# Second layer of a four-part block on one core: background pauses and rates, the ranks' third product, and a counter kept by GpSimd

## What is computed

```python
# selective scan, 512 inner channels, 16 states
x_ssm, res = split(x @ W_in.T); x_ssm = silu(causal_conv(x_ssm, taps of 4) + b_conv)
dt = softplus(x_ssm @ W_dt.T + b_dt);  B = second half of x_ssm @ W_x.T
h = exp(dt * A) * h + dt * B * x       # for each token, channel and state
y = (h.sum(states) + D * x) * silu(res);  out = y @ W_out.T
# router of the expert groups
scores = softmax(x2 @ router_w); weights, experts = top_k(scores, 2)
xs = x2[tokens sorted by expert]
```

## Time and profile before

| | |
|---|---|
| time, median of 3 runs | 5053.47 us (5053.16 to 5054.25) |
| time of the profiled execution | 5061.28 us |
| its span, first to last instruction | 5059.5 us |
| instructions | 58338 |
| busy share of the span: PE, DVE, ACT, POOL | 87%, 76%, 50%, 60% |
| second layer's scans | about 2596 to 4361 us |
| one chunk of it | 97 us (the first), then 109 to 116 us, the last 100 |

### The profile page before, as it was taken

One profiled execution on the slowest core, in us unless ns is written; L12 is line 12 of the kernel. 1 busy time (PEld: TensorE's weight loads), 2 busy tenths in 40 slices (PEclk: granted clock), 3 DMA queues, 4 the chain that ended last, 5 costly groups with the idle time before them and its releaser, 6 DMA issues.

```text
span 5059.5 us, 58338 instructions
## 1 busy us (share of the span) xinstructions
PE 4382.1 (87%) x18832; PEld 2875.0 (57%) x18832; DVE 3830.7 (76%) x6231; ACT 2543.8 (50%) x4769; POOL 3022.2 (60%) x1972
## 2 busy tenths in 40 slices
PE   4789999899899899899988888989888888489994
PEld 1355555555555555555655555555555555378883
DVE  6898767788767788766148888888888888645677
ACT  1334333334333334333557777777777766245552
POOL 4455444555444455444156888888788888745552
PEclk7899999999999999999989999999999998699997
DMA  4233332333322333322111221111122111496787
GB/s 142 84 101 110 99 96 84 100 98 109 98 90 90 98 100 107 98 89 89 57 70 55 83 74 69 71 65 64 64 82 84 64 65 65 151 237 206 252 272 279
DMA packets 302509, 545.46 MB, mean 108 GB/s; under 512 B 30592, under 2 KB 146560, under 8 KB 293248
## 3 DMA queue, kind: packets, MB, share of 16 engines
q1 hardware_dynamic: 274560, 466.08, 28.5%
q0 software_dynamic: 27648, 75.67, 4.1%
HBM read 422.71 MB, written 118.92 MB: 107 GB/s over the span
## 4 chain that ended last, share of the span: by engine, by line
PE 52%; DVE 23%; ACT 10%; POOL 7%; issue 5%; DMA 2%; SPq 0%; DVEq 0%; POOLq 0%; another core or an unknown queue 0%; ACTq 0%
PE psum L207 20%; PE psum L794 6%; DVE a_S L896 5%; PE psum L1902 5%; POOL c_dbx L1419 4%; PE psum L669 4%; DVE c_hs L1437 4%; PE psum L1161 4%; DVE a_prod L902 3%; PE psum L1453 3%; PE psum L1925 3%; PE psum L1209 2%; PE psum L918 2%; ACT psum L1426 2%; POOL sorted_rows L1376 1%
## 5 line engine op out<-in xcount | busy, mean ns | idle before, releaser
L1419 POOL TENSOR_TENSOR c_dbx<-c_dtx,c_Brep 128x1024 f32<-128x1024 f32 x512 | 1202.3, 2363 | 265.6 <-DVE c_hs L1437 210.2
L1437 DVE TENSOR_TENSOR_SCAN c_hs<-psum,c_carry,c_dbx 128x512 f32<-128x512 f32 x768 | 934.8, 1264 | 149.6 <-ACT psum L1426 117.6
L887 POOL TENSOR_TENSOR a_kv<-a_rk,a_kv 128x512 f32<-128x512 f32 x512 | 790.4, 1557 | 398.3 <-DMA a_kv<-v_rows 397.8
L813 POOL TENSOR_TENSOR a_hid_e<-a_hid_e,a_g_rep 128x512 f32<-128x512 f32 x256 | 376.8, 1475 | 868.7 <-ACT a_hid_e L802 624.4
L896 DVE TENSOR_TENSOR_SCAN a_S<-a_decay,a_carry,a_kv 128x513 f32<-128x513 f32 x512 | 813.9, 1590 | 62.6 <-POOL a_kv L887 56.6
L1426 ACT ACTIVATE psum<-c_dt,c_cols 128x512 f32<-128x512 f32 x1024 | 694.1, 687 | 297.0 <-DVE c_hs L1437 289.6
L1453 PE MATMUL psum<-ident,c_hs 128*128 128x128 f32 x4096 | 649.5, 296 | 156.7 <-DVE c_hs L1437 152.1
L1453 PEld LDWEIGHTS psum<-ident,c_hs 128*128 128x128 f32 x4096 | 515.4, 152 | 412.7 <-DVE c_hs L1437 242.1
L902 DVE TENSOR_TENSOR a_prod<-a_rk,a_S 128x512 f32<-128x512 f32 x512 | 515.0, 1006 | 186.0 <-PE psum L918 185.8
L794 PE MATMUL psum<-a_W_down,a_hid_e 128*128 128x256 f32 x2304 | 561.8, 390 | 51.0 <-DVE a_xb L826 24.2
L207 PE MATMUL psum<-a_xT,a_W_up 128*128 128x512 f32 x1152 | 557.8, 614 | 47.2 <-ACT a_hid_e L802 47.1
(11 more groups left out here) (267 smaller groups left out, 6999.5 us busy)
## 6 DMA issues: line engine op xcount, KB each, us to landing
a_kv<-v_rows SPq DMA_DIRECT2D x512, 256.0 KB
a_g_rep<-g_rows SPq DMA_DIRECT2D x256, 256.0 KB, 3.8
c_Brep<-b_rows SPq DMA_DIRECT2D x64, 1024.0 KB
d_xs<-sorted_rows SPq DMA_DIRECT2D x320, 128.5 KB
d_w<-results SPq DMA_DIRECT2D x64, 512.0 KB, 11.4
d_w<-in_d_experts SPq DMA_DIRECT2D x32, 768.0 KB
sorted_rows<-d_zeros SPq DMA_DIRECT2D x66, 128.5 KB, 11.0
a_xa<-in_L_attn_x SPq DMA_DIRECT2D x16, 512.0 KB, 4.5
```

What stands on the lines that cost most here:

```text
L887: m_kv[g] = pool.mark(nc.gpsimd.tensor_tensor(kv[:, g % NV, 1:C + 1], rk[slot][:, 1, hb, :], kv[:, g % NV, 1:C + 1], ALU.mult))
L1419: m_dbx[g] = m_dbx[g + 1] = pool.mark(nc.gpsimd.tensor_tensor(dbx[:, r:r + 2, :], dtx[slot][:, e, :].unsqueeze(1).broadcast_to([P, 2, C]), ...
L1437: m_scan[q] = dve.mark(nc.vector.tensor_tensor_scan(hs[:, q % NR, :], psum[:, DA + q % ND, :], dbx[:, q % NX, :], first, ALU.mult, ALU.add))
```

## The change

In `before`, ACT's Silu of the convolution comes `LAG + 1` = 3 background steps after PE's last product where it came 1 after, and ACT's reading of a step size 3 where it was 2. The ranks' product comes 2 steps after DVE's additions where it was 1. The rates of `after_scan` and `before` go from 1.15 and 1.15 to 1.2 and 1.3.

The expert's beginning is now added by PE: a third pair of one row of ones and `route.room`, in the bank of the ranks, except in the last chunk, where DVE adds it. With that L1355 goes, and the cast L1549 that fed it.

The number of the result row is written by DVE in the first two chunks alone. From the third on `sort_rows` waits for the transfers of two chunks before, and POOL adds a constant (`two_chunks`, set once by DVE) to what is there.

```diff
@@ before
-                yield
+                yield from pause(LAG + 1)
                 for e, i, bank, m in held:
                     act.after(m, *scanned)
                     m_xs[e] = G.freed[i] = act.mark(nc.scalar.activation(xs_[:, e, :], bank, ACT.Silu, bias=b_conv[:, e, :]))
@@ step_size
                 m = pe.mark(m)
-                yield from pause(LAG)
+                yield from pause(LAG + 1)
@@ after_scan
-            dve.mark(nc.vector.tensor_scalar(xn_[:, :, D], token_row[:, :], float(c * C * TOP), None, ALU.add))
+            if c < 2:
+                dve.mark(nc.vector.tensor_scalar(xn_[:, :, D], token_row[:, :], float(c * C * TOP), None, ALU.add))
...
-            yield
+            yield from pause(LAG)
             i, bank = yield from G.claim(pe)
...
-            m_rank = m_done["yT free", c] = pe.mark(matmuls(nc, ranks, [(tri[:, :], R["chosen"][:, :, :].rearrange("p r e -> p (r e)")),
-                                                                       (ones[:, :], ahead[:, 0:TL, :].rearrange("p t e -> p (t e)"))]))
+            pairs = [(tri[:, :], R["chosen"][:, :, :].rearrange("p r e -> p (r e)")), (ones[:, :], ahead[:, 0:TL, :].rearrange("p t e -> p (t e)"))]
+            if c < NCH - 1:
+
+                pairs.append((ones[0:1, :], route.room[0:1, :].unsqueeze(1).broadcast_to([1, TL, NE])))
+            m_rank = m_done["yT free", c] = pe.mark(matmuls(nc, ranks, pairs))
...
+                m = dve.mark(nc.vector.tensor_tensor(moved, moved, route.room[:, :].unsqueeze(1).broadcast_to([P, TL, NE]), ALU.add))
+                dve.after(m)
...
-            dve.after(m)
-            m = dve.mark(nc.vector.scalar_tensor_tensor(out=place[:, :, :, :].rearrange("p t g k -> p (t g) k"), in0=R["index_f"][:, :, :], scalar=float(Z.pitch),
-                                                        in1=place[:, :, :, :].rearrange("p t g k -> p (t g) k"), op0=ALU.mult, op1=ALU.add))
@@ sort_rows
-            pool.after_alone(*m_done["placed", c])
+            m_row = None
+            if c >= 2:
+
+                pool.engine.wait_ge(s_sorted[c % 2], c // 2 * per_chunk)
+                m_row = pool.mark(nc.gpsimd.tensor_tensor(route.xn[c % 2][:, :, D], route.xn[c % 2][:, :, D], two_chunks[:, :], ALU.add))
+            pool.after_alone(*m_done["placed", c], m_row)
@@ rates
-        AFTER_RATE, BEFORE_RATE, SORT_RATE, AHEAD = 1.15, 1.15, 0.4, 2
+        AFTER_RATE, BEFORE_RATE, SORT_RATE, AHEAD = 1.2, 1.3, 0.4, 2
@@ router
     m = dve.mark(nc.vector.tensor_copy(picks, R["index"][:, :, 0:top]))
-    dve.mark(nc.vector.tensor_copy(R["index_f"][:, :, :], R["index"][:, :, 0:top]))
```

## The result

The changed kernel takes 5024.35 us (median of 4 runs, 5021.03 to 5027.1), the kernel before 5053.86 beside it: 29.5 us less, a ratio of 0.9937 (95%: 0.9924 to 0.9951). Forecast were 5019.5 us and 34 less. The two profiled executions are 40.2 us apart (span 5059.5 and 5019.2), 32.6 of them between the first and the last scan of the second layer, where the change acts. The other 7.7 lie before and behind it, where the profiles of all these kernels differ by such amounts (the first scan starts between 2589.2 and 2601.4 us, though what stands ahead of it is the same in all), so 32.6 is what there is to explain.

What follows compares the result with a forecast made beforehand. The bound was taken to move inside a chunk: POOL nearly full first, PE from step 16 to 35, then DVE. Terms -20 - 4 - 11 - 3.5 + 5 = -33.5, say -34 us, from 5053.5 to 5019.5; range 4988 to 5048.

Steps and rivals of the forecast that it cites:

- Part 1, the reads: ScalarE's reads of PE's products sit 1 to 2 scan steps later: -20 us at the convolution, -4 at the step sizes.
- The terms of -20 and -4: Later reads: 1.3 us in 15 chunks at the convolution (bounds 0, -36), 0.3 a chunk at the step sizes (0, -15).
- rival A: ScalarE's wait for PE at the convolution only moves to the gate; DVE's edits leave -10, 5043 us; chance 0.20.
- Part 2, L1301 to L1303: DVE's L1301 removed, but L1303 behind it waits for the same end of POOL's multiplication: 0, bounds 0 and -23 us.
- Part 2, L1355 and L1549: DVE's removed instructions after step 43: L1355 -3.5 us (bounds -5, +5), cast L1549 -11 us (bounds -11, 0).
- The rates: Higher background rates hardly compress PE's work, since the second projection waits for a bank; PE's program stays as it is.
- Part 3: PE's third product for the ranks, at step 46: cost 0, hidden by DVE's work; +16 us if that cover is gone.
- Part 4: POOL's added instruction in sort_rows, 1.1 us with its wait, counting only in the first piece: +5 us, bounds 0 and +18.
- rival C: POOL becomes the bound, DVE waits for it over 25 us: slower, +18, 5071 us; chance 0.11.
- B: Cover is better: L1301's wait really vanishes, L1303 staying at 0.16, or two scans are won: about 5000 us; chance 0.17.
- D: Steps don't shift because banks run out, all parts lost in each other: within 5 us of 5053; chance 0.07.

Runs made afterwards that it cites:

- e1: Kernel before with the lengthened pauses and the rates 1.2 and 1.3, none of the edits on DVE, PE and POOL: 5063.57 us, ratio 1.0011.
- e6: Changed kernel with the result row's number written by DVE in every chunk and POOL's addition gone: 5032.04 us, ratio 0.9942 to the kernel before.
- e7: Changed kernel with the reciprocal of the total written to PSUM: 5030.73 us, ratio 0.9935 to the kernel before.
- e9: Changed kernel with reciprocal, chosen counts and places in PSUM, two small copies on ScalarE: 4997.23 us, ratio 0.9898 to the kernel before.
- e2: Changed kernel with the old pauses and rates put back, so the edits alone: 5059.28 us, ratio 1.0009 to the kernel before.
- e5: Changed kernel with the expert's beginning added by DVE again (L1355, L1549 back, PE's third product out): 5059.57 us, ratio 0.9999 to the kernel before.
- e3: Kernel before with the rates 1.2 and 1.3 alone: 5113.58 us, ratio 1.0114.
- e8: Changed kernel with the old rates, 1.15 and 1.15: 5032.37 us, ratio 0.9939 to the kernel before.
- e10: Same as e9 but with the old rates, 1.15 and 1.15: 4974.27 us, ratio 0.9856 to the kernel before.
- e4: Kernel before with the lengthened pauses alone, rates kept at 1.15: 5030.93 us, ratio 0.9948.

## Why the prediction was right, and where not

**Total and sign: right.** Forecast -34, measured -29.5 by the medians and -32.6 in the stretch. The terms stand less well.

**Part 1, the reads: size right, place partly wrong.** The exponentials sent before each read are now 27 and 37 at the convolutions, 40 and 44 at the gate, 47, 50, 54, 57 at the step sizes (before: 26 and 35, 39 and 43, and the same four). That is the count by hand, step for step. The terms of -20 and -4 stand against 240.2 - 215.2 = 25 us of idle time won, and e1 shows it without the edits (27). By place, DVE's idle time in all chunks fell from 82.8 to 28.7 us behind the scans 32 to 35, where the second convolution is read, and rose by 19 behind 36 to 39, by 6 behind 40 to 43 and by 10 behind 12 to 15. The convolution's wait fell to 14.5, as forecast under 35. But the gate's wait did not grow (11.0 to 7.0). I had overlooked the read between the two gates: the B projection's copy stays at 41 exponentials, while the first gate's read ahead of it comes one later. Its place in the changed kernel, in the timelines of ScalarE, PE and DVE:

```profile
3292.09 0.69 ACT L1434 ACTIVATE psum<-c_dt,c_cols 128x512 f32<-128x512 f32 x1
3294.51 0.57 ACT L1199 COPY c_tmp<-psum 16x512 f32<-16x512 f32 x1 [1.73 <-PE psum L207]
```

```profile
3290.86 3.61 PE L207 MATMUL psum<-c_xs,c_W_B 128*16 128x512 f32 x8
```

```profile
3295.70 1.28 DVE L1445 TENSOR_TENSOR_SCAN c_hs<-psum,c_carry,c_dbx 128x512 f32<-128x512 f32 x1 [0.97 <-ACT psum L1434]
```

ScalarE has sent one exponential since the gate and stands 1.73 us until PE's product is over at 3294.47; DVE then stands 0.97. DVE's wait for exponentials fell further than forecast (108 for 145), and the difference was given back: where ScalarE is no longer late PE is, and DVE waits for its transposes at step 36 (23.3 us) and for the output projection at step 16 (12.3 us). That is rival A's mechanism in small, at three places that I had not named.

**Part 2, L1301 to L1303: right.** The wait passed to the next instruction as forecast, 2.6 to 24.6 us, and e6 puts it, together with POOL's addition, at nothing (ratio 0.9942 for 0.9937). This is the rule of the Trainium skill that the prediction drew on ("SBUF — State Buffer", section "Who interferes with whom": an exclusive lock on the shared ports, taken by two SBUF inputs or by copy and cast in a two-port mode). e7 and e9 agree with it: the same operation took 0.17 us with one input in PSUM and, in most of its places, 1.85 with two in SBUF, both 0.53 to 0.55 us behind POOL's start.

**Part 2, L1355 and L1549: near as a difference of two kernels, mis-sized as parts.** Forecast -3.5 and -11. Between the two profiles the lines that the edits touch fell by about 18 us (L1301 -21.2, L1549 -12.7, L1355 -5.8, the weights +22.0, the cast to the row -1.0, the comparison behind L1549 +0.9), -14.5 being forecast, and DVE's busy time, in which neighbours that overlap count once, by 7.6. By themselves the edits are worth nothing with the old timing (e2), their 11 us coming back as idle time, while with the new timing (e5) L1355 and L1549 are worth all 30. The weak step is the costing of each part by the durations of the kernel before. I took L1355 at 5.8 us though one long case showed that its length is a matter of when it comes (there is a second, 1.32 us at 4353.24); the pauses, in the same change, moved it, and it would have taken 28.0 (e1). So the parts don't add up: pauses and rates alone 1.0011, edits alone 1.0009, both 0.9937. The total came out near because L1355 is gone in the changed kernel, and with it what the pauses do to it, and because the instructions behind it do not wait (e5). Of this the prediction weighed only the cast behind L1355, so that much is luck. The instructions' own work is only 7.7 us (14 and 16 of them at 0.16, 16 at 0.17).

**The rates.** I held them for neutral because the bank claims pin PE's program. e3 refutes that for ScalarE: the rates pull its reads forward, by up to four exponentials, at a cost of 55 us. PE's program is pinned up to the second convolution only (its last products come when 34 scans have begun, for 35 before); the step sizes' products begin at 40 for 43. In the changed kernel the rates make up for the longer pauses and are not needed (e8).

**Part 3: right.** The third product stands nowhere in the waits; DVE's wait for the places' bank is 4.0 us. PE's wait for the counts fell from 29.4 to 2.2 instead of staying; I take that to be without effect, as DVE is full there.

**Part 4: too high.** The addition is 0.21 us and its wait 9.9 us in 11 times, 0.9 each as forecast, but the 5 us of cost do not show: without it (e6) the idle time is 1.5 us less. DVE's waits for POOL went from 13.7 to 18.1, under the 25 of rival C.

**The rivals.** B's L1303 at 0.16 did not come, C did not decide, D fell. A holds in part, as said.

Open: how much of e10's further 23 us is the later reads, how much the other spread of PE's work that e4 showed, and how much TensorE's clock, below.

## What to carry to other kernels

A small DVE instruction that meets a long GpSimd one costs what its place and its operands make it, not what its size says; look for short forms with long durations, and for the next such form behind them, before a removal is costed. Removing such an instruction hands the wait on where the next one is of a waiting form (L1301 to L1303, L1304 to the copy), and ends it where the next ones have an operand in PSUM (L1355); giving every small form in reach such an operand ended it everywhere but in two instructions. Where an in-order engine reads another's results, try delaying the reads before raising the rate of the background, and time changes of order and edits together: here the pauses with their rates, and the edits, were each worth nothing alone.

## What the runs showed of the hardware

The size of a contending instruction hardly matters: 128x4, 128x16 and 128x64 forms all stood until POOL's end (1.96 us at 0.41 us behind its start, 1.86 at 0.53, 1.77 at 0.63). In 107 places, in ten profiles, a scalar_tensor_tensor of 128x16 with two inputs in SBUF began between 0.42 us ahead of POOL's multiplication and 1.42 behind its start; every one of them ended 2.37 to 2.42 us behind that start. A reciprocal of 128x8 within SBUF stayed at 0.19 us through POOL's multiplications: in the changed kernel the one at 3298.78 began 1.72 us behind POOL's start and 0.64 ahead of its end. POOL's indirect DMA instruction, 1.03 us long, did not hold DVE: in the changed kernel L1304 took 0.17 us at 4083.41, with that instruction running from 0.15 us before to 0.87 behind its start, and 33 such places in the profiles show 0.17 to 0.26 us.

TensorE's granted clock differs with how the background is spread: its mean over the execution is 0.930 before, 0.932 in the changed kernel and 0.943 in e10. Windows at the end of the same chunk, before (steps 56 to 59, 60 to 63, and 0 to 3 of the next) and then e10 (the same steps), columns as in the earlier trace rows:

```profile
3348.77:3354.67 5.90, 2.62 (x16) 1.68 (x16) 5.90 (x8) 4.71 (x10) 5.71 (x4) 1.00 0.58 200
3354.67:3361.18 6.51, 4.00 (x16) 2.56 (x16) 6.37 (x14) 3.38 (x8) 4.85 (x3) 0.57 0.80 261
3361.18:3366.46 5.28, 5.01 (x24) 4.78 (x24) 5.28 (x7) 3.35 (x6) 4.97 (x4) 0.56 0.00 0
```

```profile
3308.75:3314.63 5.88, 5.88 (x27) 3.46 (x26) 5.88 (x7) 5.85 (x11) 4.71 (x2) 1.00 0.07 26
3314.63:3320.77 6.14, 6.14 (x28) 3.53 (x27) 6.02 (x7) 6.11 (x13) 4.68 (x2) 1.00 0.66 252
3320.77:3327.25 6.48, 4.71 (x30) 3.23 (x28) 6.48 (x8) 6.29 (x12) 5.03 (x3) 1.00 0.00 0
```

Before, PE had 2.62 us of work in the 5.90 us of the first window, and the clock then stood near its lower level of 1.2 GHz (0.57, 0.56). In e10 the background reaches into the next chunk, PE was full in the first two windows, and the clock stayed at 2.4 GHz. Over the whole stretch of the scans the same number of recorded PE passes, 7446, took 1545.2 us of busy time in the changed kernel and 1507.1 in e10. DVE is full in these steps, so nearly nothing of it shows there; what it gives elsewhere was not separated from the later reads.
